# Third attention layer: a software-pipelined loop is made two steps deeper, with the head norms one step later and all that follows them two steps later

## The chip, the core and the metric

The kernel runs on one core of a Trainium2 chip, in one launch. Its time is the device time of that launch in microseconds (us). The core has five instruction streams that run side by side and meet only at semaphores: TensorE (PE in the profile; its weight loads stand apart as PEld), VectorE (DVE), ScalarE (ACT), GpSimd (POOL) and SyncE (SP). Each stream executes in the order in which it is written, so an instruction that waits holds up all that stands behind it on its engine.

## The reference, cut to what matters

The model has four layers of attention and feed-forward network (FFN) over x of 8 x 128 tokens x 256 features. The change is in the attention of the third layer (`_L2_xattn_ref`), which is:

```python
ln_out = _ln(hidden_states, ln_w, ln_b)
q  = _ln(fp8_linear(ln_out, wq), qln_w, qln_b)      # 16 heads of 128
k  = _ln(fp8_linear(ln_out, wk), kln_w, kln_b)      # 8 groups of 128
v  = fp8_linear(ln_out, wv)
core = gqa(q, k, v)                                 # softmax(q k / sqrt(128)) v
qx = _ln(fp8_linear(ln_out, wqx), qxln_w, qxln_b)
kx, vx = split(cond @ w_kv_x.T); kx = _ln(kx, kxln_w, kxln_b)
xout = gqa(qx, kx, vx)
cat = concatenate([core, xout])
return (div_clamp_fp8(cat, proj_smooth) @ wproj.T) * (proj_in_scale * proj_w_scale)
```

Each head of q, k, qx and kx is layer-normalised on its own (the head norms).

## The kernel before, in words

`attention_l2` quantises the layer's input first and then runs one long loop, in which all engines work on several **items** at once. An item is a pair (b, side): batch element b of 8, side 0 the self attention (q, k, v) and side 1 the attention over the context (qx, kx, vx). There are 16 items, in the order (0,0), (0,1), (1,0) and so on. Each item has 8 **steps** t = 0 to 7, and every engine's program goes through the same steps in the same order; `phases` (line 1345) calls each engine's `fn` with the item that enters (`pi`), the one before it (`ai`) and the one before that (`zi`), with two empty items at either end. What stands at a step is laid out by hand with a lag in steps, counted from t = 0 of `pi`:

- PE projects one block of 512 columns at each t into PSUM tile `l2x_pr` (line 1420 in bf16, six matmuls; line 1425 in f32, four matmuls, at t = 0, 1, 6, 7 of side 1).
- ACT copies it out (line 1488), to `l2x_raw` for t = 0 to 5 (two blocks of keys, four of queries) and to `v`, shown as x_normT, for t = 6, 7.
- DVE takes the moments of block t (`bn_stats`, line 1540). POOL combines them for two blocks at a time, at t = 1, 3, 5, with nine small operations and a power (lines 1389 to 1399; x^-0.5).
- `norm_due` with lag 3: DVE normalises block u at step u + 3 (line 1550, four instructions, one a head). With lag 4: PE transposes the block (line 1440) into the one tile `l2x_tr`, and ACT copies it out with the affine of the norm (line 1502) to `kT` or `qT`.
- `due` places the work of a quarter a = 0 to 3 of an item (4 heads), every second step, counted from t = 0 of `ai`: scores on PE (lag 0, line 1433), their maximum on DVE (lag 0, line 1545), exp on ACT (lag 1, line 1493), the reciprocal of the sum on DVE (lag 2, line 1556), the product with it on POOL (lag 2, line 1403), transposes of the probabilities on PE and their copy on ACT (lag 4, lines 1447 and 1507), values on PE and their copy on ACT (lag 5, lines 1454 and 1514), rounding to fp8 on DVE (lag 6, lines 1564 and 1216 to 1218) and POOL (lag 7, line 1380), and the output projection into `l2x_y` on PE (lag 9, line 1465).
- At the end of side 1 DVE adds the output to x (line 1571), behind its step 7 of `zi`.

Where several things fall on one step, each engine has a fixed order. DVE: moments, maximum, normalise, reciprocal, rounding. PE: projection, scores, transposes of the norm, transposes of the probabilities, values, output. ACT: copy of the projection, exp, affine, copy of the probabilities, copy of the values. The dual tiles (`pr`, `s`, `p`, `pT`, `of`, `step`, `wide`) are used in turns; credits (line 42) fill the semaphores beforehand.

```python
if job := norm_due(t, 4, pi, ai):
    _, u, l = job
    pe.wait_ge(s["normed"], l + 1)
    pe.wait_ge(s["affined"], l + 1)
```

Of the kernel before, what the change touches and what calls it, by code (L numbers as in the profile page):

```python
# [12 lines left out]
ALU = mybir.AluOpType  # L13
# [4 lines left out]
D = 256  # L18
KD = D // P
B = 8  # L20
# [1205 lines left out]
def attention_l2(pg, pre):  # L1226


    nc, G, DH = pg.nc, 8, 128
# [5 lines left out]
    with outer:  # L1235
# [71 lines left out]
        s = {m: pg.sem(f"l2x_{m}") for m in names}  # L1307
        with ExitStack() as st:
# [36 lines left out]
            def phases(fn):  # L1345
                items = [None, None] + [(b, side) for b in range(B) for side in range(2)] + [None, None]
                for i in range(2, len(items)):
                    fn(items[i], items[i - 1], items[i - 2])
# [8 lines left out]
            def due(t, lag, ai, zi):  # L1357

                for it, at in ((ai, t), (zi, t + 8)):
                    a, odd = divmod(at - lag, 2)  # L1360
                    if it is not None and not odd and 0 <= a < 4:
                        return it, a, item(it) * 4 + a
                return None
# [5 lines left out]
            def _(pool):  # L1369
# [5 lines left out]
                def fn(pi, ai, zi):  # L1375
                    for t in range(8):
                        if job := due(t, 7, ai, zi):
                            _, a, m = job
                            pool.wait_ge(s["widened"], m + 3)
                            nc.gpsimd.tensor_tensor(cq[:, a], wide[:, a % 2], step[:, a % 2], ALU.subtract).then_inc(s["quanted"], 1)  # L1380
# [19 lines left out]
                        if job := due(t, 2, ai, zi):  # L1400
                            _, a, m = job
                            pool.wait_ge(s["recip"], m + 1)
                            nc.gpsimd.tensor_tensor(p[:, a % 2], p[:, a % 2], rsm[:, a % 2].unsqueeze(2).to_broadcast([P, U, P]),  # L1403
                                                    ALU.mult).then_inc(s["p_normed"], 1)
# [3 lines left out]
            def _(pe):  # L1408
                def fn(pi, ai, zi):
                    for t in range(8):  # L1410
# [17 lines left out]
                        if job := due(t, 0, ai, zi):  # L1428
                            it, a, m = job
                            pe.wait_ge(s["affined"], item(it) * 6 + a + 4)  # L1430
                            pe.wait_ge(s["exped"], m + 1)
                            for j in range(U):
                                last = nc.tensor.matmul(s_ps[a % 2][:, j, :], qT[:, it[1], a, j, :], kT[:, it[1], 2 * a + j // 2, :], start=True, stop=True)
                            last.then_inc(s["scores"], 1)
                        if job := norm_due(t, 4, pi, ai):
                            _, u, l = job
                            pe.wait_ge(s["normed"], l + 1)
                            pe.wait_ge(s["affined"], l + 1)
                            for j in range(U):
                                last = nc.tensor.transpose(tr[:, j, :], raw[:, u, j, :], pg.ident[:])  # L1440
                            last.then_inc(s["ln_turned"], 1)
                        if job := due(t, 4, ai, zi):
                            _, a, m = job
                            pe.wait_ge(s["p_normed"], m + 1)
                            pe.wait_ge(s["p_kept"], m + 1)
                            for j in range(U):
                                last = nc.tensor.transpose(pt[:, j, :], p[:, a % 2, j, :], pg.ident[:])
                            last.then_inc(s["p_turned"], 1)
                        if job := due(t, 5, ai, zi):
# [7 lines left out]
                        if job := due(t, 9, ai, zi):  # L1457
# [13 lines left out]
            def _(act):  # L1471
# [8 lines left out]
                def fn(pi, ai, zi):  # L1480
                    for t in range(8):
# [7 lines left out]
                        if job := due(t, 1, ai, zi):  # L1489
# [6 lines left out]
                        if job := norm_due(t, 4, pi, ai):  # L1496
# [7 lines left out]
                        if job := due(t, 4, ai, zi):  # L1504
                            _, a, m = job
                            act.wait_ge(s["p_turned"], m + 1)
                            nc.scalar.activation(flat(pT[:, a % 2]), flat(pt[:]), ACT.Copy).then_inc(s["p_kept"], 1)
                        if job := due(t, 5, ai, zi):
# [10 lines left out]
            def _(dve):  # L1519
# [14 lines left out]
                def fn(pi, ai, zi):  # L1534
                    for t in range(8):
                        if pi is not None and t < 6:
# [5 lines left out]
                        if job := due(t, 0, ai, zi):  # L1542
# [3 lines left out]
                        if job := norm_due(t, 3, pi, ai):  # L1546
# [6 lines left out]
                        if job := due(t, 2, ai, zi):  # L1553
# [3 lines left out]
                        if job := due(t, 6, ai, zi):  # L1557
# [9 lines left out]
                    if zi is not None and zi[1] == 1:  # L1567
                        b = zi[0]
                        dve.wait_ge(s["y_done"], b + 1)
                        xb = pg.x[:, b, :]  # L1570
                        nc.vector.scalar_tensor_tensor(out=xb, in0=y[:, 0:D], scalar=yscale[:], in1=xb, op0=ALU.mult, op1=ALU.add).then_inc(s["y_added"], 1)
# [796 lines left out]
```

## Time and profile before

| | |
|---|---|
| median of 3 runs | 1958.79 us (1957.7 to 1960.71) |
| the profiled execution | 1962.16 us, of which its span 1960.4 us |
| mean granted clock of PE | 0.854 of full speed |
| the loop that is changed | from 969 to 1420 us of the span |
| one item in the middle of the loop | 26.86 us (322.3 us for 12 items) |

The span is what lies between the first and the last recorded instruction. Lines named Lnnn are lines of the kernel. "Busy" of an engine leaves its waits out; a duration in which an instruction is held up after its start is counted as busy. Other stages stand before and after the loop: the FFN of the second layer before it, a layer norm and the FFN of the third layer behind it.

### The profile page before, as it was taken

The page shows a single profiled execution, that of the slowest core. Times are in us where ns is not written, and L with a number is a line of the kernel's source. Part 1 is how long each engine was busy: PE and PEld are TensorE (multiplying, and loading weights), DVE is VectorE, ACT ScalarE, POOL GpSimd, SP SyncE. Part 2 cuts the span into 40 slices and gives each one's busy share as a digit, 9 for nine tenths or more (in the row PEclk, how much of TensorE's full clock was granted, in tenths as well). Part 3 has the DMA queues.
Part 4 walks back from the last instruction along what each step waited for, and adds up shares of the span by engine and source line. Part 5 has one row for each costly group of instructions (what it writes and reads, how often), then busy time and mean ns, then how long its engine had stood idle before and what let it go on. Part 6 is the DMA issues. An engine that isn't in the chain of part 4 may idle for free. (4 is left out here: it accounts for less than half of the span.)

```text
span 1960.4 us, 25164 instructions
## 1 busy us (share of the span) xinstructions
PE 1622.0 (83%) x8434; PEld 1001.9 (51%) x8472; DVE 1139.4 (58%) x2581; ACT 820.9 (42%) x1887; POOL 772.1 (39%) x1036
## 2 busy tenths in 40 slices
PE   6688878999686799997189999999799989837772
PEld 5323335556453455555056666666555565535551
DVE  5788872222644732424779999999832245562335
ACT  2888873110322211112477777787631111412221
POOL 0266651000200187910466777777610000016672
PEclk9755557999688799998599999999989987957896
DMA  2198871110500313110200000000011110056656
GB/s 73 44 170 164 161 152 63 41 32 25 172 1 12 146 59 127 51 62 2 85 1 2 1 2 1 2 1 1 1 59 33 41 32 1 4 209 213 212 167 236
DMA packets 174224, 140.12 MB, mean 71 GB/s; under 512 B 141793, under 2 KB 154721, under 8 KB 170386
## 3 DMA queue, kind: packets, MB, share of 16 engines
q1 hardware_dynamic: 165314, 114.89, 20.7%
q0 software_dynamic: 6416, 22.03, 3.4%
q10 hardware_dynamic: 2368, 1.61, 0.3%
q8 instruction: 69, 1.13, 0.3%
q14 instruction: 57, 0.47, 0.1%
HBM read 85.43 MB, written 19.50 MB: 54 GB/s over the span
## 5 line engine op out<-in xcount | busy, mean ns | idle before, releaser
L1811 POOL CAST l0m_pi<-l0m_pf 128x1024 bf16<-128x1024 int16 x128 | 133.2, 1040 | 136.3 <-ACT l0m_pf L1878 135.4
L350 PE MATMUL l1e_gu<-x_normT,l1e_w 128*128 128x512 f32 x384 | 170.8, 599 | 0.0
L1905 DVE TENSOR_REDUCE l0m_mx<-l0m_s 128x1 f32<-128x1024 f32 x128 | 155.8, 1217 | 25.0 <-PE l0m_s L1820 24.0
L1420 PE MATMUL l2x_pr<-l_w,l2x_xq 128*128 128x512 bf16 x538 | 134.4, 386 | 42.9 <-ACT credits L42 40.5
L1878 ACT ACTIVATE l0m_pf<-l0m_s,l0m_bias,l0x_sq 128x1024 int16<-128x1024 f32 x128 | 154.0, 1204 | 33.0 <-DVE l0m_bias L1909 26.9
L1820 PE MATMUL l0m_s<-l0x_kT,l0x_qT 48*128 48x512 bf16 x256 | 124.0, 622 | 31.9 <-ACT l0m_pf L1878 26.5
L1550 DVE TENSOR_SCALAR l2x_raw<-l2x_raw,l2x_mv,l2x_rs 128x128 f32<-128x128 f32 x384 | 147.9, 446 | 3.3 <-POOL l2x_rs L1399 3.3
L350 PE MATMUL l0e_gu<-x_normT,l0e_w 128*128 128x512 f32 x272 | 121.6, 602 | 0.0
L350 PEld LDWEIGHTS l1e_gu<-x_normT,l1e_w 128*128 128x128 f32 x384 | 73.8, 193 | 83.8 <-issue 82.8
L350 PE MATMUL l2e_gu<-x_normT,l2e_w 128*128 128x512 f32 x256 | 114.2, 601 | 0.0
L426 DVE TENSOR_TENSOR l1e_h<-l1e_sil,l1e_gu 128x512 f32<-128x512 f32 x40 | 27.5, 687 | 132.9 <-ACT l1e_sil L402 132.9
L1540 DVE BATCH_NORM_STATS2 l2x_bn<-l2x_raw 128x6 f32<-128x128 f32 x384 | 83.1, 278 | 36.2 <-ACT l2x_raw L1488 36.1
L1420 PEld LDWEIGHTS l2x_pr<-l_w,l2x_xq 128*128 128x128 bf16 x576 | 57.1, 99 | 91.6 <-ACT credits L42 40.5
L402 ACT ACTIVATE l1e_sil<-l1e_gu 128x512 f32<-128x512 f32 x48 | 28.6, 596 | 178.6 <-PE l1e_gu L350 178.6
L1403 POOL TENSOR_TENSOR x_norm<-x_norm,l2x_rsm 128x512 f32<-128x512 f32 x64 | 76.5, 1195 | 63.9 <-DVE l2x_rsm L1556 63.8
L1493 ACT ACTIVATE x_norm<-l2x_s,l2x_mx 128x128 f32<-128x128 f32 x256 | 90.0, 370 | 1.0 <-DVE l2x_mx L1545 0.9
L1380 POOL TENSOR_TENSOR l2x_cq<-ctx_tok,l2x_step 128x512 bf16<-128x512 f32 x64 | 74.2, 1159 | 38.6 <-DVE ctx_tok L1218 38.6
L1440 PE MATMUL l2x_tr<-ident,l2x_raw 128*128 128x128 f32 x384 | 61.9, 284 | 30.7 <-DVE l2x_raw L1550 30.3
L357 PE MATMUL l1e_y<-l1e_w,l1e_h 128*128 128x256 f32 x384 | 86.1, 379 | 0.0
L426 DVE TENSOR_TENSOR l0e_h<-l0e_sil,l0e_gu 128x512 f32<-128x512 f32 x28 | 19.2, 688 | 110.7 <-ACT l0e_sil L402 110.7
L350 PEld LDWEIGHTS l0e_gu<-x_normT,l0e_w 128*128 128x128 f32 x272 | 52.5, 194 | 60.0 <-issue 59.3
L357 PEld LDWEIGHTS l1e_y<-l1e_w,l1e_h 128*128 128x128 f32 x384 | 73.0, 190 | 18.5 <-issue 9.6
(515 smaller groups left out, 3635.3 us busy)
## 6 DMA issues: line engine op xcount, KB each, us to landing
l3m_w<-in_l_moe SPq DMA_DIRECT2D x16, 1280.0 KB, 6.7
l1e_w<-in_l_ffn SPq DMA_DIRECT2D x24, 384.0 KB, 3.2
l_rows<-zero_row SPq DMA_DIRECT2D x8, 1024.0 KB, 11.1
l_w<-l_rows SPq DMA_DIRECT2D x8, 1024.0 KB, 11.9
l0e_w<-in_l_ffn SPq DMA_DIRECT2D x17, 384.0 KB, 3.1
l2e_w<-in_l_ffn SPq DMA_DIRECT2D x16, 384.0 KB, 3.1
ctx_tok<-l_route SPq DMA_DIRECT2D x8, 512.0 KB
l2q_wps<-in_l_wp SPq DMA_DIRECT2D x16, 256.0 KB, 2.8
```

Source lines behind the costliest of these rows:

```text
L350: last = nc.tensor.matmul(gu[half][:, m, :], w[:, c % SW, (2 * k + m) * P:(2 * k + m + 1) * P], pg.xnT[:, k, cols(n)], start=(k == 0), sto ...
L357: last = nc.tensor.matmul(y[:, t, :], h[:, c % SH, t * P:(t + 1) * P], w[:, c % SW, WG:CHUNK], start=(c == 0 and t % 2 == 0), stop=False, ...
L1380: nc.gpsimd.tensor_tensor(cq[:, a], wide[:, a % 2], step[:, a % 2], ALU.subtract).then_inc(s["quanted"], 1)
L1403: nc.gpsimd.tensor_tensor(p[:, a % 2], p[:, a % 2], rsm[:, a % 2].unsqueeze(2).to_broadcast([P, U, P]), ALU.mult).then_inc(s["p_normed"], 1)
L1420: last = nc.tensor.matmul(flat(pr[t % 2][:]), src[:, k, tokens], pg.l2_w3[:, part, k, at:at + W], start=(k == 0 and part == 0), stop=(k == ...
L1493: last = nc.scalar.activation(p[:, a % 2, j, :], s_ps[a % 2][:, j, :], ACT.Exp, bias=mx[:, a % 2, j:j + 1], accum_out=sm[:, a % 2, j:j + 1])
L1540: last = nc.vector.bn_stats(bn[:, t, j, :], raw[:, t, j, :])
L1550: last = nc.vector.tensor_scalar(raw[:, u, j, :], raw[:, u, j, :], mv[:, u, j, 0:1], rs[:, 1, u, j:j + 1], ALU.subtract, ALU.mult)
L1811: nc.gpsimd.tensor_copy(pi[:, n % 8, :], pf[:, n % 4, :]).then_inc(s["rounded"], 1)
L1820: last = nc.tensor.matmul(s_ps[n % 3][:, g * HALF:(g + 1) * HALF], qT[:, h, b * P:(b + 1) * P], kT[:, h, g * HALF:(g + 1) * HALF], start=T ...
L1878: nc.scalar.activation(pf[:, n % 4, :], s_ps[n % 3][:], ACT.Exp, scale=sq[:, b, h:h + 1], bias=bias[:, n % 4:n % 4 + 1], accum_out=sm[:, b ...
L1905: nc.vector.tensor_reduce(mx[:, n % 4:n % 4 + 1], s_ps[n % 3][:], AX, ALU.max).then_inc(s["maxed"], 1)
```

## The change

Every lag of `due` on every engine is raised by 2, so that scores, softmax, values, rounding and output of an item come two steps later against its projections. Of the head norms, DVE's normalise goes from lag 3 to lag 4, and PE's transposes and ACT's affine from lag 4 to lag 6. The last lag is then 11 and its last quarter falls at step 17 of `ai`, so a fourth item `wi` is handed through, and there are three empty items at either end. DVE's addition to x moves from behind step 7 of `zi` to the start of step 2 of `wi`. No instruction, tile or buffer is added or taken away. The head of every `fn` gets the fourth argument.

```diff
             def phases(fn):
-                items = [None, None] + [(b, side) for b in range(B) for side in range(2)] + [None, None]
-                for i in range(2, len(items)):
-                    fn(items[i], items[i - 1], items[i - 2])
+                items = [None] * 3 + [(b, side) for b in range(B) for side in range(2)] + [None] * 3
+                for i in range(3, len(items)):
+                    fn(items[i], items[i - 1], items[i - 2], items[i - 3])
...
-            def due(t, lag, ai, zi):
+            def due(t, lag, ai, zi, wi):
...
-                for it, at in ((ai, t), (zi, t + 8)):
+                for it, at in ((ai, t), (zi, t + 8), (wi, t + 16)):
...
             def _(pool):
...
-                        if job := due(t, 7, ai, zi):
+                        if job := due(t, 9, ai, zi, wi):
...
-                        if job := due(t, 2, ai, zi):
+                        if job := due(t, 4, ai, zi, wi):
...
             def _(pe):
...
-                        if job := due(t, 0, ai, zi):
+                        if job := due(t, 2, ai, zi, wi):
...
-                        if job := norm_due(t, 4, pi, ai):
+                        if job := norm_due(t, 6, pi, ai):
...
-                        if job := due(t, 4, ai, zi):
+                        if job := due(t, 6, ai, zi, wi):
...
-                        if job := due(t, 5, ai, zi):
+                        if job := due(t, 7, ai, zi, wi):
...
-                        if job := due(t, 9, ai, zi):
+                        if job := due(t, 11, ai, zi, wi):
...
             def _(act):
...
-                        if job := due(t, 1, ai, zi):
+                        if job := due(t, 3, ai, zi, wi):
...
-                        if job := norm_due(t, 4, pi, ai):
+                        if job := norm_due(t, 6, pi, ai):
...
-                        if job := due(t, 4, ai, zi):
+                        if job := due(t, 6, ai, zi, wi):
...
-                        if job := due(t, 5, ai, zi):
+                        if job := due(t, 7, ai, zi, wi):
...
             def _(dve):
...
                     for t in range(8):
+                        if wi is not None and wi[1] == 1 and t == 2:
+                            b = wi[0]
+                            dve.wait_ge(s["y_done"], b + 1)
+                            xb = pg.x[:, b, :]
+                            nc.vector.scalar_tensor_tensor(out=xb, in0=y[:, 0:D], scalar=yscale[:], in1=xb, op0=ALU.mult, op1=ALU.add).then_inc(s["y_added"], 1)
...
-                        if job := due(t, 0, ai, zi):
+                        if job := due(t, 2, ai, zi, wi):
...
-                        if job := norm_due(t, 3, pi, ai):
+                        if job := norm_due(t, 4, pi, ai):
...
-                        if job := due(t, 2, ai, zi):
+                        if job := due(t, 4, ai, zi, wi):
...
-                        if job := due(t, 6, ai, zi):
+                        if job := due(t, 8, ai, zi, wi):
...
-                    if zi is not None and zi[1] == 1:
-                        b = zi[0]
-                        dve.wait_ge(s["y_done"], b + 1)
-                        xb = pg.x[:, b, :]
-                        nc.vector.scalar_tensor_tensor(out=xb, in0=y[:, 0:D], scalar=yscale[:], in1=xb, op0=ALU.mult, op1=ALU.add).then_inc(s["y_added"], 1)
```

## Rows read from the trace of the kernel before

**Rows 1.** Windows: busy time of each engine in 12 items of the loop

```profile
core 0: us, PE busy (x) PEld busy (x) DVE busy (x) ACT busy (x) POOL busy (x), PEclk, DMA share, GB/s
1069.00:1391.30 322.30, 300.02 (x1746) 209.68 (x1773) 296.98 (x872) 252.40 (x794) 235.61 (x456) 1.00 0.00 1
```

**Rows 2.** Who waited for whom, 1069 to 1391.3 us: total, times, longest

```profile
PEld l2x_tr L1440 <- DVE l2x_raw L1550: 38.1, 48, 1.3
...
DVE l2x_bn L1540 <- ACT l2x_raw L1488: 20.0, 24, 1.2
PE l2x_tr L1440 <- DVE l2x_raw L1550: 19.8, 24, 1.1
```

**Rows 3.** The same for steps 0+1, 2+3, 4+5, 6+7 of one side-1 item

```profile
1149.66:1156.51 6.85, 6.80 (x41) 4.75 (x41) 5.67 (x18) 5.44 (x19) 2.22 (x2) 1.00 0.00 0
1156.51:1161.76 5.25, 5.25 (x34) 3.77 (x34) 4.37 (x16) 4.30 (x16) 4.86 (x13) 1.00 0.01 2
1161.76:1169.34 7.58, 6.55 (x36) 4.25 (x36) 7.48 (x23) 5.69 (x19) 6.56 (x14) 1.00 0.01 2
1169.34:1176.59 7.25, 7.17 (x44) 5.18 (x44) 7.08 (x19) 5.38 (x19) 6.01 (x12) 1.00 0.00 0
```

**Rows 4.** The same for the whole side-0 item behind it

```profile
1176.59:1203.39 26.80, 24.36 (x148) 17.08 (x149) 24.89 (x73) 21.26 (x67) 19.62 (x38) 1.00 0.00 1
```

**Rows 5.** Timeline of PE around that item's step 4, and at a step 0

```profile
1163.23 0.66 PE L1440 MATMUL l2x_tr<-ident,l2x_raw 128*128 128x128 f32 x4 [0.97 <-DVE l2x_raw L1550]
1163.72 0.60 PE L1447 MATMUL l2x_pt<-ident,x_norm 128*128 128x128 f32 x4
...
1203.93 0.60 PE L1440 MATMUL l2x_tr<-ident,l2x_raw 128*128 128x128 f32 x4
1204.37 0.60 PE L1447 MATMUL l2x_pt<-ident,x_norm 128*128 128x128 f32 x4
```

**Rows 6.** DVE alone, between the maxima of steps 0, 2, 4, 6, 0

```profile
1151.14:1158.08 6.94, 5.66 (x19) 1.00 0.00 0
1158.08:1163.88 5.80, 5.70 (x20) 1.00 0.01 1
1163.88:1170.23 6.35, 6.18 (x19) 1.00 0.01 3
1170.23:1178.15 7.92, 7.18 (x19) 1.00 0.00 0
```

**Rows 7.** Timeline: DVE's normalise and POOL's wide operations in the same stretches

```profile
1160.19 1.24 POOL L1403 TENSOR_TENSOR x_norm<-x_norm,l2x_rsm 128x512 f32<-128x512 f32 x1
1161.23 1.94 DVE L1550 TENSOR_SCALAR l2x_raw<-l2x_raw,l2x_mv,l2x_rs 128x128 f32<-128x128 f32 x4
1161.39 1.19 POOL L1380 TENSOR_TENSOR l2x_cq<-ctx_tok,l2x_step 128x512 bf16<-128x512 f32 x1
...
1168.78 1.39 DVE L1550 TENSOR_SCALAR l2x_raw<-l2x_raw,l2x_mv,l2x_rs 128x128 f32<-128x128 f32 x4
...
1170.84 1.11 DVE L1550 TENSOR_SCALAR l2x_raw<-l2x_raw,l2x_mv,l2x_rs 128x128 f32<-128x128 f32 x4
```

**Rows 8.** Timeline from the exp of one step 1 to the next exp, ACT and DVE

```profile
1207.21 0.36 ACT L1493 ACTIVATE x_norm<-l2x_s,l2x_mx 128x128 f32<-128x128 f32 x1
...
1210.24 0.75 ACT L1488 ACTIVATE l2x_raw<-l2x_pr,l2c_scales 128x512 f32<-128x512 f32 x1
1211.03 0.87 DVE L1540 BATCH_NORM_STATS2 l2x_bn<-l2x_raw 128x6 f32<-128x128 f32 x4 [1.17 <-ACT l2x_raw L1488]
1211.82 0.67 DVE L1545 TENSOR_REDUCE l2x_mx<-l2x_s 128x4 f32<-128x512 f32 x1
```

**Rows 9.** Timeline: the addition to x on DVE

```profile
1176.26 0.47 DVE L1571 SCALAR_TENSOR_TENSOR x_res<-l2x_y,l2x_yscale,x_res 128x256 f32<-128x256 f32 x1
```

**Rows 10.** A pair of steps while the loop fills, and two pairs while it drains

```profile
991.22:998.22 7.00, 6.78 (x39) 4.23 (x38) 3.36 (x13) 5.30 (x14) 1.99 (x10) 1.00 0.00 0
1397.91:1405.08 7.17, 5.80 (x42) 4.86 (x41) 6.21 (x13) 6.04 (x26) 3.73 (x4) 1.00 0.00 1
```

More of the change, by code:

```diff
@@ L1373, in _, with fn @@
                 AGGR = 9
-                def fn(pi, ai, zi):
+                def fn(pi, ai, zi, wi):
                     for t in range(8):
-                        if job := due(t, 7, ai, zi):
+                        if job := due(t, 9, ai, zi, wi):
                             _, a, m = job
@@ L1408, in _, with fn @@
             def _(pe):
-                def fn(pi, ai, zi):
+                def fn(pi, ai, zi, wi):
                     for t in range(8):
@@ L1478, in _, with fn @@
                 act.wait_ge(s["smooth"], 1)
-                def fn(pi, ai, zi):
+                def fn(pi, ai, zi, wi):
                     for t in range(8):
@@ L1532, in _, with fn @@
                 QSTEPS = 3
-                def fn(pi, ai, zi):
+                def fn(pi, ai, zi, wi):
                     for t in range(8):
+                        if wi is not None and wi[1] == 1 and t == 2:
[3 more added lines that the diff above has]
+                            nc.vector.scalar_tensor_tensor(out=xb, in0=y[:, 0:D], scalar=yscale[:], in1=xb, op0=ALU.mult, op1=ALU.add).then_inc(s["y_added"], 1)
                         if pi is not None and t < 6:
```

## The prediction

> **What bounds the kernel now.** I read the page's tenths first, to find where this loop lies, and then three views of it: busy time by windows, the waits, and the timeline. In the middle of the loop 12 items take 322.3 us, 26.86 us each, with PE busy for 300.02 us (25.0 an item) and DVE for 296.98 us (24.75), while ACT and POOL have more room, and the granted clock is 1.00 [rows 1]. So no engine is full, but two are within 8% of it: what is lost is 1.86 us an item on PE and 2.1 us on DVE. The waits say how. PE waits 24 times, 19.8 us in all (1.65 us an item), to transpose a block that DVE has not yet normalised; its weight loads wait 38.1 us for the same. DVE waits 24 times, 20.0 us, for ACT's copy of a projection, and that copy comes from PE [rows 2]. The two hold each other up.
>
> The place shows by pairs of steps. Steps 2 and 3 carry no transposes of a norm and take 5.25 us, with PE busy all the time. Steps 4 and 5 take 7.58 us, of which PE works 6.55 [rows 3]. The missing 0.97 us is the wait of the first transpose, at 1163.23 us [rows 5]. It stands for the normalise that began at 1161.23 and took 1.94 us [rows 7]. PE wants the block one step after DVE may begin it, and DVE reaches each step some 2 us after PE.
>
> **The change, part by part.** All work keeps its amount; only its distance in steps changes.
>
> *Transposes 2 steps behind the normalise instead of 1.* This adds a step, some 3.2 us (26.86 / 8 is 3.36), to a distance that lacks 0.97 us now, so 2.2 us are left over and PE's 1.65 us an item go. What is late next: the transposes of the probabilities wait for POOL's product. In the same pair of steps the product ends at 1160.19 + 1.24 = 1161.43 us [rows 7] and PE takes it at 1163.72 [rows 5], after its own 0.97 us of waiting. Without that wait 1.3 us of slack is left. This is enough for the mean, not for every disturbance.
>
> *Normalise one step later.* The steps of DVE that carry one change from 0, 3, 4, 5, 6, 7 to 0, 1, 4, 5, 6, 7. Counted from maximum to maximum DVE is busy 5.66, 5.70, 6.18 and 7.18 us [rows 6]. The four instructions of a normalise take 1.11 us undisturbed, 1.03 in a row with others (0.08 overlaps), and 0.28 more where they meet the end of a POOL operation (1.39) [rows 7]. The first stretch becomes 5.66 + 1.03 + 0.28 = 6.97 us. The second loses the disturbed one of 1.94 us: 3.76 us. So the load becomes less even: 6.97, 3.76, 6.18, 7.18.
>
> *What keeps DVE from using the light stretch.* Exp needs the maximum, and on ACT the exp, the affine and the copy of the values stand ahead of the next projection's copy, which DVE's moments and next maximum need. From the exp at 1207.21 us it goes to the copy at 1210.24, the moments at 1211.03, the maximum at 1211.82 plus 0.67 [rows 8]: 5.28 us, with 0.1 us for the handover 5.4 us. No stretch can be shorter. DVE's round is then 6.97 + 5.4 + 6.18 + 7.18 = 25.73 us in an item with the addition to x, and 0.4 less in one without (it takes 0.47 us [rows 9], less the overlap).
>
> *PE's round.* Its transposes move from steps 0, 1, 4 to 7 to steps 0 to 3, 6, 7; the amount stays. They cost 0.44 us a block (1203.93 to 1204.37 us) [rows 5]. PE is busy 6.80 + 5.25 + 6.55 + 7.17 = 25.77 us in a side-1 item [rows 3] and 24.36 us in a side-0 item [rows 4].
>
> *The sum an item.* Side 1: the larger is PE's 25.77. Side 0, into which the addition to x now falls (step 2 of `wi`): DVE's 25.73. The mean is 25.75. To it I add 0.2 us, what PE waits today for other causes (1.86 - 1.65). That gives **25.95 us an item** against 26.86: 0.91 us less, and over the 15 items that enter with scores running 13.7 us less.
>
> *The addition to x, moved.* It waits for PE's last output matmul. Before, PE issues that in step 7 and DVE adds behind its own step 7. Now they are step 1 and the head of step 2, and PE's next use of the tile is at step 3 where it was step 1: the same distances. It costs nothing, since DVE runs behind PE: the present one starts with no wait [rows 9]. If DVE caught up with PE it would wait at most for that group of matmuls, under 1 us every second item, with the moments, the maximum and all of DVE's step 2 behind it.
>
> *Depth.* The loop has two steps more. One pair of the fill stays without scores. Such a pair was 7.00 us when the first scores fell into it, PE busy 6.78 [rows 10]; without its scores and the load of exp's table I take 4.6 (bounds 4.0 and 7.0). One full pair of 26.86 / 4 = 6.7 us goes, and the drain gains a pair: two of them take 7.17 us [rows 10], 3.6 each. That is 4.6 - 6.7 + 3.6 = +1.5 us. Norms and transposes that now reach further into the drain add about 1 us (one normalise of 1.03 us exposed; bounds 0 and 2). Together +2.5 us, between +0.4 and +6.
>
> **Sum:** -13.7 + 2.5 = -11.2 us. Against the profiled execution of 1962.2 us (span 1960.4 and 1.8 around it) this gives 1951.0. That execution lies 3.4 us over the median of the runs, 1958.8, so for a median I predict **1947.6 us**.
>
> **A rule to set beside the rows.** The normalise of four instructions takes 1.11 us undisturbed and 1.94 us while POOL's product (1160.19 to 1161.43 us) and rounding (from 1161.39) run [rows 7]; DVE stands still meanwhile, and its busy time holds that. The Trainium skill (SBUF — State Buffer, section "SBUF: two separate sides") says that DVE and GpSimd share a port pair which one of them holds for a whole instruction while the other is blocked. By that rule a DVE without gaps meets more of POOL's operations. The trace agrees with the block itself (1.94 against 1.11 us).
>
> **The rivals.**
>
> *A. The wait simply goes.* PE's 1.65 us an item vanish and DVE keeps up: 25.2 us an item. 15 x 1.65 = 24.8 us less, 2.5 more: 1936.5 us. For it: PE's other waits are small [rows 1, 2]. Against it: DVE's 24.75 us busy would have to fit almost without a gap. Chance 0.17.
>
> *B. POOL in DVE's way.* DVE's gaps (20.0 us in 12 items [rows 2]) now let POOL's rounding pass. If they go, the normalises of steps 1 and 5 are held for 0.83 us each (1.94 - 1.11) instead of 0.28: 1.1 us an item more on DVE. With PE partly above it in side 1, some 0.65 of it reaches the item: 26.6 us, 15 x 0.26 = 3.9 less, 2.5 more: 1957.4 us, no change that can be told. The rule above would work this way. Against it: at step 1 today DVE has a gap of 1.17 us [rows 8] that POOL may use, and part of it stays, as the light stretch is bound by ACT. Chance 0.18.
>
> *C. Slower: the uneven rounds don't even out.* PE and DVE may stay tied pair by pair, now by POOL's product (1.3 us slack). Then each pair costs the larger of the two. PE's side-1 pairs become 6.80, 6.11, 5.69, 7.17 (two transposes of 0.43 moved from the third to the second), and DVE's are 6.97, 5.4, 6.18, 7.18: the maxima sum to 26.44. The same sum for today is 6.80 + 5.70 + 6.55 + 7.18 = 26.23, and the item really takes 26.93 [rows 3], 0.7 more. If those 0.7 remain, the item takes 27.14 us: 0.28 more, x 15 = 4.2, and 2.5 for depth: 1965.5 us. It decides from the point where DVE cannot be 2 us behind PE after steps 4 to 1 without PE waiting. For it: DVE's heavy stretches now follow each other (6.18, 7.18, 6.97), 20.3 us in which PE needs 19.7. Against it: 1.3 us of slack covers that difference of 0.6. Chance 0.15.
>
> **How the numbers follow.** My forecast has 0.50, with a range of its own from 1942 to 1954: the depth's bounds give -2 and +3.5, and 0.2 us more or less an item 3 each way. About 0.2% (4 us) is what a measurement of this kernel can tell from no change: the border of faster is 1954.9, of slower 1962.7. Faster: the forecast, A, and 0.04 of B's spread, less 0.01 of the forecast's own tail, 0.70. Slower: C, 0.15. The same: the rest, 0.15. The range from 1936 to 1961 takes in A's centre, the forecast and B, and leaves out C (0.15) and what lies below A's centre (some 0.05).
>
> **What would show it.** Right: in the waits, "PE l2x_tr for DVE l2x_raw L1550" falls from 24 in 12 items to a handful. Steps 4 and 5 come down from 7.6 us to about 6, while steps 2 and 3 rise from 5.25 us to about 6. DVE's stretch from step 2 to 4 is the one with an idle time (about 1.6 us), waiting for ACT; an item takes about 26 us. The last maximum to the end of the loop is unchanged, the drain one pair longer. B would show as more than 1.39 us for the normalises of steps 1 and 5, with DVE busy over 25.5 us an item; C as PE waiting for POOL L1403 at its transposes of the probabilities. I am wrong if an item stays near 26.9 us, or if the waits for the normalise remain.

## The result: 1927.8 us, 31 us faster

| | before | after |
|---|---|---|
| median | 1959.22 us (1957.70 to 1960.71, 4 runs) | 1927.78 us (1926.58 to 1929.21, 4 runs) |
| ratio | | 0.9837 (95% interval 0.9822 to 0.9851) |
| profiled execution | 1962.16 us, span 1960.4 | 1926.58 us, span 1924.8 |
| the loop, first projection to last addition | 451.5 us | 427.3 us |
| 12 items in its middle | 322.4 us | 305.7 us |
| its first three items | 73.1 us | 60.9 us |
| its last item and the drain | 56.0 us | 60.6 us |
| the rest of the span | 1508.9 us | 1497.5 us |

The direction was forecast, the size was not: I gave 1947.6 us, from 1936 to 1961. The loop alone gave 24.2 us where 11.2 were forecast, and the profiled executions differ by a further 11.4 us in stages that the change doesn't touch. An item is counted from the start of ACT's first copy (line 1488) of it to that of the next, except that the first one begins with the loop.

The middle of the loop after the change, busy time by engine (the columns of [rows 1]), and its waits:

```profile
1025.60:1331.30 305.70, 296.58 (x1747) 209.86 (x1777) 285.35 (x870) 253.12 (x794) 236.37 (x457) 1.00 0.00 1
```

```profile
DVE l2x_bn L1545 <- ACT l2x_raw L1488: 15.4, 12, 1.3
PEld l2x_tr L1440 <- DVE l2x_raw L1555: 14.1, 24, 1.2
ACT x_norm L1493 <- DVE l2x_mx L1550: 12.7, 18, 1.2
...
PE l2x_tr L1440 <- DVE l2x_raw L1555: 5.3, 12, 0.7
...
PE l2x_pt L1447 <- POOL x_norm L1403: 1.8, 6, 0.3
```

PE is busy 97% of the time, against 93% in [rows 1]. Its wait for the normalise (now line 1555; the moments are line 1545 and the maximum line 1550) fell from 19.8 us to 5.3 us. DVE is busy 11.6 us less for nearly the same instructions, mainly because they are held up for less time after their start: the normalises take 5.9 us less (below) and the last step of the rounding (line 1218) 3.5 us less.

DVE alone between the maxima of the steps that were 0, 2, 4, 6 and 0 in [rows 6] (now 2, 4, 6, 0 and 2), over two items:

```profile
1130.33:1137.31 6.98, 6.88 (x24) 1.00 0.01 2
1137.31:1142.61 5.30, 3.91 (x16) 1.00 0.00 2
1142.61:1148.66 6.05, 5.95 (x20) 1.00 0.00 0
1148.66:1155.46 6.80, 6.70 (x20) 1.00 0.01 2
1155.46:1162.84 7.38, 7.28 (x25) 1.00 0.00 1
1162.84:1168.14 5.30, 3.91 (x15) 1.00 0.01 3
1168.14:1174.50 6.36, 6.26 (x19) 1.00 0.00 0
1174.50:1181.31 6.81, 6.71 (x20) 1.00 0.00 0
```

The second stretch is the light one: 3.91 us of work in 5.30 us, each time. All others are full. So DVE sets the pace, except in that stretch, where its next moments wait for ACT.

### The profile page after: what moved, and what is told of

It is laid out like the page before. It is cut to its first block and busy times, and to the rows that moved or that the text cites. A ratio compares the mean times of both kernels' runs of the same rounds, so it can differ in the third digit from the quotient of the medians.

```text
span 1924.8 us, 25164 instructions
## 1 busy us (share of the span) xinstructions
PE 1602.1 (83%) x8434; PEld 993.4 (52%) x8472; DVE 1120.4 (58%) x2581; ACT 821.3 (43%) x1887; POOL 773.6 (40%) x1036
## 5 line engine op out<-in xcount | busy, mean ns | idle before, releaser
L1555 DVE TENSOR_SCALAR l2x_raw<-l2x_raw,l2x_mv,l2x_rs 128x128 f32<-128x128 f32 x384 | 141.7, 429 | 1.6 <-POOL l2x_rs L1399 1.5
L350 PE MATMUL l0e_gu<-x_normT,l0e_w 128*128 128x512 f32 x272 | 121.7, 602 | 0.0
L1399 POOL TENSOR_TENSOR l2x_rs<-l2x_rs,l2x_half 128x8 f32<-128x8 f32 x48 | 83.4, 1737 | 3.8
```

What stands on the lines that cost most here:

```text
L350: last = nc.tensor.matmul(gu[half][:, m, :], w[:, c % SW, (2 * k + m) * P:(2 * k + m + 1) * P], pg.xnT[:, k, cols(n)], start=(k == 0), sto ...
L1399: g.tensor_tensor(rs[:, 1, two, :], var, half[:, 0], ALU.pow).then_inc(s["rstd"], 1)
L1555: last = nc.vector.tensor_scalar(raw[:, u, j, :], raw[:, u, j, :], mv[:, u, j, 0:1], rs[:, 1, u, j:j + 1], ALU.subtract, ALU.mult)
```

## The experiments

The ratios are to the kernel before, run in the same group. The groups of runs differ: the kernel before took 1957.5, 1977.3, 1957.9 and 1979.9 us (medians) in the four of them. In r_before 18 us of this lie behind the first matmul of the fourth layer's expert stage (264.1 us to the end, against 246.1 us in the first profile); the cause is open. So kernels of different groups are compared by ratio, and by the time of their loop.

| run | ratio, 95% interval | loop | first 3 items | 12 items | rest |
|---|---|---|---|---|---|
| kernel before | 1 | 451.5 | 73.1 | 322.4 | 56.0 |
| changed kernel | 0.9837 [0.9822, 0.9851] | 427.3 | 60.9 | 305.7 | 60.6 |
| e1 depth only | 1.0004 [0.9989, 1.0019] | 451.8 | 71.6 | 322.4 | 57.7 |
| e2 transposes at lag 5, no depth | 0.9939 [0.9923, 0.9956] | 440.0 | 65.6 | 318.1 | 56.2 |
| e3 normalise 3, transposes 6 | 0.9900 [0.9884, 0.9917] | 433.1 | 61.6 | 312.0 | 59.5 |
| e4 normalise 4, transposes 5 | 1.0009 [1.0000, 1.0019] | 461.1 | 70.3 | 328.6 | 62.1 |
| r_before | 0.9998 [0.9988, 1.0009] | 450.1 | 73.1 | 322.5 | 54.5 |
| r_after | 0.9829 [0.9811, 0.9847] | 427.3 | 60.9 | 305.7 | 60.7 |
| e5 normalise 4, transposes 7 | 0.9886 [0.9866, 0.9906] | 426.1 | 60.0 | 305.6 | 60.5 |
| e6 normalise 5, transposes 7 | 0.9891 [0.9874, 0.9907] | 429.3 | 61.5 | 307.6 | 60.2 |
| e7 one short memset more | 0.9889 [0.9872, 0.9907] | 427.5 | 60.9 | 305.9 | 60.7 |
| e8 six memsets more | 0.9854 [0.9836, 0.9873] | 427.4 | 60.9 | 305.8 | 60.7 |
| e9 normalise 3, moments first | 1.0105 [1.0087, 1.0123] | 474.5 | 66.6 | 348.5 | 59.4 |
| e10 one step of depth | 0.9935 [0.9902, 0.9967] | 438.2 | 67.4 | 313.0 | 57.8 |
| e11 normalise 3, no power | 0.9820 [0.9793, 0.9846] | 417.7 | 59.6 | 300.1 | 58.0 |
| e12 changed kernel, no power | 0.9852 [0.9832, 0.9872] | 427.3 | 60.8 | 305.7 | 60.8 |

### Which of the three moves makes the gain

**Depth alone (e1).** The lags of `due` as in the change, the head norms as before:

```diff
-                        if job := norm_due(t, 4, pi, ai):   # DVE
+                        if job := norm_due(t, 3, pi, ai):
-                        if job := norm_due(t, 6, pi, ai):   # PE, ACT
+                        if job := norm_due(t, 4, pi, ai):
```

> Only the lags of scores to output are raised by 2 and the fourth item is in flight; normalise stays at lag 3, transposes and affine at lag 4. Theory (the distance between normalise and transposes makes the gain): PE still waits for DVE's normalise some 1.6 us an item, an item stays at 26.7 to 27.0 us, and the kernel takes about 1958 to 1962 us. Rival (the depth itself, more distance between projections and scores, makes the gain): an item falls to 25.5 us and the time to about 1930 us.

The 12 items take 322.4 us, the same as before to 0.1 us, with the same waits:

```profile
PEld l2x_tr L1440 <- DVE l2x_raw L1555: 38.1, 48, 1.3
...
PE l2x_tr L1440 <- DVE l2x_raw L1555: 19.9, 24, 1.1
DVE l2x_bn L1545 <- ACT l2x_raw L1488: 19.1, 24, 1.2
```

So depth gives nothing by itself, and costs little: the loop is 0.3 us longer (1.5 less in the fill, 1.7 more at the end), or 1.7 us against the loop of r_before, which had a faster end (54.5 us).

**Depth and the later normalise, but the old distance of one step (e4).** `norm_due(t, 5, ...)` on PE and ACT in the changed kernel.

> The changed kernel with transposes and affine at lag 5, one step behind the normalise as before the change. Theory (distance): PE's waits for the normalise come back (15 us or more in 12 items), an item takes 26.5 to 27.2 us, the time 1948 to 1962 us. Rival (depth or the new place of the normalise makes the gain): an item stays near 25.5 us, the time near 1930 us.

The waits are back, worse than before the change, and 12 items take 328.6 us. The upper end that I gave, 27.2 us an item, was still too low (27.4):

```profile
PEld l2x_tr L1440 <- DVE l2x_raw L1555: 44.4, 48, 1.6
DVE l2x_bn L1545 <- ACT l2x_raw L1488: 35.3, 24, 2.1
...
PE l2x_tr L1440 <- DVE l2x_raw L1555: 25.8, 36, 1.1
```

e1 and e4 together show that the gain stands or falls with the second step between normalise and transposes. Depth is its room: at transposes of lag 6 block 2 is turned at step 0 of `ai`, and PE's scores of the first quarter, which need it, would stand ahead of it at the old lag 0.

**The distance alone, without depth (e2).** The kernel before with one edit, on PE and ACT:

```diff
-                        if job := norm_due(t, 4, pi, ai):
+                        if job := norm_due(t, 5, pi, ai):
```

> The kernel before with one edit: transposes and affine at lag 5 instead of 4, that is two steps behind the normalise, no extra depth; the affine of a quarter's last block is then one step ahead of its scores instead of two. Theory (distance makes the gain): an item falls to 25.2 to 25.7 us, and the time to 1926 to 1940 us. Rival (the distance from the affine to the scores is needed as well): PE waits for ACT's copy l2x_qT at its scores (L1433), an item stays above 26.3 us, the time above 1948 us.

The kernel gains 0.6%, where the change gains 1.6%, and neither account holds: the time is 1945.77 us and an item takes 26.5 us, but not for the reason that the rival gave. The waits in its middle 12 items name another engine:

```profile
PE l2x_pt L1447 <- POOL x_norm L1403: 14.2, 12, 1.5
...
DVE l2x_raw L1550 <- POOL l2x_rs L1399: 12.3, 12, 1.0
```

PE now waits for POOL's product, and DVE's normalise waits for POOL's power. Neither wait stands in the middle of the loop in the kernel before.

### Why the normalise has to be later too

**Normalise back at lag 3 (e3),** the rest as in the change:

```diff
-                        if job := norm_due(t, 4, pi, ai):   # DVE
+                        if job := norm_due(t, 3, pi, ai):
```

> The changed kernel with DVE's normalise back at lag 3, transposes at lag 6 (three steps apart). Theory of the prediction (moving the normalise makes DVE's load uneven, and the light stretch from the maximum of step 2 to that of step 4 idles 1.3 us): the idle time in that stretch goes, an item falls from 25.5 to about 25.1 us, the time by some 5 us to 1922. Rival (the disturbances by POOL grow where the normalise then falls, at step 3): an item stays at 25.5 us or above and the time at 1928 us or above.

The first account, the prediction's, fell: 12 items take 312.0 us, 6.3 more than with lag 4. The rival's range came (26.0 us an item, 1937.88 us), but its reason, POOL's disturbances, is only a part. The timeline of POOL, DVE and PE in steps 2 to 4 of a side-1 item shows why:

```profile
1088.91 0.21 POOL L1389 TENSOR_TENSOR l2x_rs<-l2x_bn 128x8 f32<-128x8 f32 x1
...
1091.78 1.64 POOL L1399 TENSOR_TENSOR l2x_rs<-l2x_rs,l2x_half 128x8 f32<-128x8 f32 x1
...
1093.38 1.04 POOL L1403 TENSOR_TENSOR x_norm<-x_norm,l2x_rsm 128x512 f32<-128x512 f32 x1
1093.45 2.68 DVE L1555 TENSOR_SCALAR l2x_raw<-l2x_raw,l2x_mv,l2x_rs 128x128 f32<-128x128 f32 x4 [1.03 <-POOL l2x_rs L1399]
1094.38 1.16 POOL L1380 TENSOR_TENSOR l2x_cq<-ctx_tok,l2x_step 128x512 bf16<-128x512 f32 x1
1094.47 0.66 PE L1447 MATMUL l2x_pt<-ident,x_norm 128*128 128x128 f32 x4 [0.92 <-POOL x_norm L1403]
```

POOL combines the moments of steps 0 and 1 from 1088.91 us on, and its power ends at 1093.42. DVE has reached step 3 by then and has waited 1.03 us. POOL's product, whose reciprocal was ready at 1089.9 us, stood behind the power too, and PE waits 0.92 us for it. Then DVE's four instructions meet the product and the rounding and take 2.68 us instead of 1.11.

**Is it POOL's power, or DVE's collisions?** In e9 I put POOL's combination of the moments ahead of its rounding at the same step.

> The run with normalise at lag 3 and transposes at lag 6 (312.0 us for 12 items, PE waiting 13.3 us for POOL's product) with one edit more: POOL combines the moments ahead of its rounding at the same step, instead of behind it. Theory (with normalise at lag 3 the faster loop is held by POOL's combination of moments, which ends in its power and stands before both DVE's normalise at step 3 and POOL's own product): that chain starts some 0.4 us sooner (the moments were ready at 1088.4 us and POOL began at 1088.9), and 12 items take 2 to 6 us less than 312.0. Rival (the cost of lag 3 is DVE's uneven load and its collisions): 12 items stay at 312 us or grow, since the rounding comes later to PE.

The first fell: 348.5 us for 12 items. The rival's range came, but by its side remark: the rounding now stands behind the power, and PE waits for it at the output projection, 30.9 us in some 250 us of the loop (its clock also fell to half four times for 3.4 us in these items). An edit that hands the delay to another consumer doesn't tell the two causes apart. So the power's time itself was taken away, at lag 3 (e11) and at lag 4 (e12). These kernels leave out the reciprocal of the standard deviation; all else stays:

```diff
-                            g.tensor_tensor(rs[:, 1, two, :], var, half[:, 0], ALU.pow).then_inc(s["rstd"], 1)
+                            g.tensor_tensor(rs[:, 1, two, :], var, half[:, 0], ALU.mult).then_inc(s["rstd"], 1)
```

> Normalise at lag 3, transposes at lag 6, and POOL's power (x^-0.5, 1.64 us, 3 an item) replaced by a product of the same tiles (about 0.2 us), so that the standard deviations are not computed and the time alone is read. Theory (POOL's combination of moments holds DVE's normalise at step 3 and its own product behind it): the waits for l2x_rs and for POOL's product go, and 12 items take 303 to 307 us instead of 312.0. Rival (DVE's collisions and uneven load cost at lag 3): 12 items stay at 310 us or more.

> The changed kernel with the power replaced in the same way. Theory (at lag 4 POOL's combination is hidden already): 12 items take 303 to 306 us instead of 305.7, so at most half of what the same edit gives at lag 3. Rival (POOL holds the loop at lag 4 as well): 12 items take under 302 us.

At lag 3 it gives 11.9 us in 12 items (312.0 to 300.1, below the 303 that I gave as the lower end), at lag 4 nothing (305.7 both). Without the power, at lag 3 and at lag 4:

```profile
1029.30:1329.30 300.00, 297.82 (x1755) 211.44 (x1784) 295.07 (x871) 251.75 (x793) 183.94 (x456) 1.00 0.00 1
```

```profile
1030.00:1335.70 305.70, 295.36 (x1748) 208.66 (x1778) 294.93 (x871) 253.39 (x793) 181.32 (x456) 1.00 0.00 1
```

```profile
DVE l2x_bn L1545 <- ACT l2x_raw L1488: 5.8, 12, 0.6
```

So POOL's power is what lag 3 costs once PE no longer waits elsewhere. That lag 4 hides it is seen best in the waits: DVE waits 6 times, 6.2 us, for `l2x_rs` in e3 and never in the 12 items of the changed kernel. The 305.7 us of e12 are a net value, for the edit also moves POOL's product onto DVE's line 1216, which takes 49.5 us there against 22.8, and DVE is busy 9.6 us more in all. And the prediction's own argument is in e11 and e12: DVE is busy alike (295.07 and 294.93 us), but at lag 4 it waits 5.8 us for ACT's copy and at lag 3 not at all, which is about the 5.6 us between them. It is the smaller of two effects.

**More distance (e5, e6).** Transposes at lag 7; in e6 the normalise at lag 5 as well.

> The changed kernel with transposes and affine at lag 7, three steps behind the normalise. Theory (two steps are enough, since DVE and ACT set the pace): PE's last waits for the normalise (5.3 us in 12 items) go, but an item stays at 25.3 to 25.5 us, the time within 3 us of the changed kernel. Rival (the remaining waits still cost): an item falls to 25.0 us, the time by 5 us or more.

> The changed kernel with both moved one step further: normalise at lag 5, transposes and affine at lag 7. The distance of two steps stays, and the distance of the normalise to POOL's power grows. DVE's steps with a normalise are then 0 to 2 and 5 to 7. Theory (lag 4 already hides POOL's power, and what counts beyond that is where the normalise falls against the other work of DVE): no wait for POOL's l2x_rs here either, the light stretch moves from step 2 to 4 to the stretch from 2 to 6, an item takes 25.3 to 26 us, no gain. Rival (more distance from POOL still pays): an item falls below 25.2 us.

e5: 305.6 us in 12 items, as with lag 6. PE's waits for the normalise are gone, and it gives nothing, since DVE and ACT set the pace. Its median missed what I gave: 1954.50 us is 8.9 more than r_after's in the same group, though the loop is 1.2 us shorter; most of it is in the clock, told below. e6: 307.6 us, no gain either.

**Half the depth (e10).** All lags of `due` one lower than in the change.

> The changed kernel with scores and all that follows one step sooner (lags 1, 3, 5, ... 10: one step deeper than before the change, not two), normalise at lag 4 and transposes at lag 6 as in the change; the addition to x one step sooner. Theory (the distance between normalise and transposes makes the gain, depth is only the room for it, and the affine one step ahead of its scores is enough): an item takes 25.3 to 25.8 us, fill and drain half a pair less, and the loop is within 3 us of the 427.3 us of the changed kernel. Rival (the place of the scores against the other work counts: scores, maximum, reciprocal and rounding now fall on the odd steps on which POOL also combines the moments): an item takes over 26 us.

The theory fell: 12 items take 313.0 us, the loop 438.2. Its waits in the middle:

```profile
DVE l2x_bn L1545 <- ACT l2x_raw L1488: 22.0, 24, 1.6
PEld l2x_pt L1447 <- POOL x_norm L1403: 20.3, 24, 1.4
DVE l2x_mx L1550 <- PE l2x_s L1433: 18.9, 12, 2.0
```

The scores and what follows them now share their steps with other neighbours. DVE collides much less (busy 266.5 us in 12 items, 18.9 less than in the changed kernel), and waits more. The range that the rival gave (over 26 us an item) is what came. Which of the shifted neighbours does it was not taken apart.

### The part of the gain outside the loop

The kernel before and the changed one, unchanged, once more in another group of runs:

> The kernel before, unchanged, once more. In the first profiles the changed kernel is 35.6 us shorter, of which the loop gives 24.2 us, and 11.4 us lie in stages that the change doesn't touch (4.5 before the loop, 6.7 in the fourth layer's attention, whose first 20.5 us ran at half of PE's clock in the kernel before and only 6.8 us in the changed one). Theory (the outside part varies from one execution to the next, as the clock does): the outside part of this execution, 1508.9 us then, comes out several us different, and the loop takes 451.5 us again within 0.5. Rival (it belongs to the kernel): 1508 to 1510 us outside, and again some 20 us at half clock.

> The changed kernel, unchanged, once more, on the same chip as the kernel before. Theory (outside varies): the loop takes 427.3 us within 0.5, the outside part, 1497.5 us in the first profile, differs by several us, and the two kernels' medians differ by 24 to 30 us. Rival (it belongs to the kernel): 1496 to 1499 us outside and medians 31 us or more apart.

The changed loop repeats (427.3 us). That of the kernel before takes 450.1 us, 1.4 less than before and outside the 0.5 that I allowed; the difference is in its end, where PE's clock stood at half for 3.4 us in the first profile and not in this one. The medians are again 30.5 us apart (1976.10 and 1945.62; 31.7 by all runs of the kernel before in the group, 1977.33), so 6 to 9 us beyond the loop's 23 to 24 come back in the medians. The two profiled executions are only 23.9 us apart: outside the loop they take 1520.4 and 1519.3 us, since this time the changed kernel entered its loop 4.7 us later. So neither account came whole.

What returns in both pairs lies where the clock does. I count from the last matmul of line 350, the gate and up projection of the third layer's FFN; 13.8 us of matmuls of line 357 follow it (the expectation of e7 calls it the FFN's last matmul, which it isn't), and then PE is idle for 6.7 us, in which the clock falls. These are the windows that begin 17 us behind that matmul (PEclk stands third from the end), of the kernel before:

```profile
1605.30:1612.30 7.00, 3.42 (x14) 2.76 (x15) 6.15 (x28) 4.69 (x10) 0.00 (x0) 0.50 0.42 140
1612.30:1626.30 14.00, 13.22 (x44) 9.61 (x43) 9.76 (x17) 2.26 (x3) 2.86 (x19) 0.52 0.04 11
```

and of the changed one:

```profile
1576.80:1583.80 7.00, 3.42 (x14) 2.77 (x15) 6.16 (x28) 4.69 (x10) 0.00 (x0) 0.51 0.42 140
1583.80:1597.80 14.00, 13.22 (x58) 7.99 (x57) 11.95 (x22) 2.26 (x3) 2.86 (x19) 1.00 0.04 11
```

Both run the same instructions after the same idle stretch. Before, PE stays at 1.2 GHz (0.5) for 20.5 us; after, it is back at 2.4 GHz after 6.8 us. From that matmul to the first of the fourth layer's expert stage it is 126.0 us before (123.6 in r_before) and 118.9 us after, in both of its profiles. All 16 profiles sort by the moment at which the clock fell behind that matmul: at 16.5 to 16.9 us the stretch takes 125.8 to 126.0 us (the kernel before, e5, e6), at 17.0 to 17.2 us 118.9 to 119.9 us (the changed kernel twice, e4, e8, e12), at 17.3 to 17.8 us 123.3 to 123.6 us (r_before, e1, e2, e3, e7, e9, e10, e11).

Is the 118.9 the changed kernel's own, or a moment that it happens to hit? e7 and e8 add memsets on DVE behind the loop:

```diff
                 phases(fn)
+                nc.vector.memset(z[:], 0.0)          # e7; e8: raw[:, u] for u in range(6)
```

> The changed kernel with one short extra DVE instruction behind the loop (a memset of the dead tile z, 512 bf16 columns, some 0.1 to 0.3 us). Between the end of the third layer's FFN and the fourth layer's expert stage the profiles so far show 118.9 us where the granted clock fell 17.0 us after the FFN's last matmul (both profiles of the changed kernel), 125.7 to 126.0 us where it fell at 16.5 to 16.9 us, and 123.3 to 123.5 us at 17.3 to 17.8 us. Theory (what the change gains outside the loop is the clock's step, hit or missed by where the loop ends): the clock now falls 0.1 to 0.5 us sooner against the stage, the stretch takes 126 us, and the kernel is 5 to 7 us slower than the changed one, for an instruction of 0.3 us or less. Rival (the changed kernel has these 7 us for itself): 118.9 us again, the time 0.3 us more.

> The changed kernel with six extra DVE memsets of 512 f32 columns behind the loop (some 1.5 to 3.5 us). Theory (the clock's step): the time grows by those us plus or minus up to 7 us, according to the moment at which the clock falls; the stretch behind the FFN takes one of the values seen, 118.9, 123.5 or 126 us, and it follows that moment as in the other profiles. Rival: the stretch keeps 118.9 us whatever that moment is, and the time grows by the length of the memsets alone.

The one memset takes 0.27 us. The stretch is at 123.3 us again, 4.4 us longer, and from the loop's end to the FFN's last matmul of line 350 it is 2.9 us more (170.8 against 167.9 us), of which 0.27 are the memset: 7.3 us for an instruction of 0.27. In that first part too the clock differs: behind the loop it stood at half for 23.9 us on end, and in the changed kernel for 10.3 and 6.8 us with 3.4 us at full between. The median is 1936.68 us against 1927.78. The six memsets take 2.9 us and cost less than the one: the median is 1931.16 us, with the stretch back at 118.9 us. The window of 14 us that shows it, of e7 and of e8:

```profile
1587.70:1601.70 14.00, 13.22 (x50) 8.51 (x49) 10.78 (x19) 2.26 (x3) 2.86 (x19) 0.75 0.04 11
```

```profile
1590.10:1604.10 14.00, 13.22 (x58) 7.97 (x57) 11.95 (x22) 2.26 (x3) 2.86 (x19) 1.00 0.06 11
```

E8's six memsets move the stages by another amount, and the clock fell 17.0 us behind that matmul, as in the changed kernel; in e7 it fell at 17.4. The expected 126 us for e7 was wrong in its value (the clock fell later, not sooner), but the claim held for this stretch: what the change gains there is a moment hit, and one instruction of 0.27 us takes it away. Only one execution of each run was profiled, so for the 6 to 9 us in the medians the clock is the likely cause, not one that was followed in every execution.

## Why the prediction was wrong, step by step

**What bounds the kernel: right.** PE's wait for the normalise was the cause. It fell from 19.8 to 5.3 us in 12 items, and only the runs with two or more steps between normalise and transposes gained anything. Two signs came as given: steps 4 and 5 of a side-1 item came down from 7.58 to 5.52 us, and steps 2 and 3 rose from 5.25 to 6.09. The waits fell to 12, not to a handful.

**The stretches of DVE: right to 0.4 us.** Forecast 6.97, 5.4, 6.18, 7.18. Measured 6.98, 5.30, 6.05 and 6.80, and in the item behind 7.38, 5.30, 6.36, 6.81. The light stretch bound by ACT came as worked out, with its idle time of 1.4 us. The 7.18 us still held the addition to x, which now runs at 1161.66 us, in the 7.38 us: it moved from one stretch to another and changes no sum.

**The sum an item: 25.95 forecast, 25.48 measured.** Two terms were too large. The first is "the larger of the two engines, item by item": PE's 25.77 us of a side-1 item, read while PE still waited, are no bound. In the changed kernel PE is busy 25.35 us in such an item (1125.35 to 1150.89 us) and 24.11 in the one behind it, 24.7 in the mean (296.58 / 12). DVE's round for both, 25.73 and 0.4 less, gives 25.53, near what came. Why PE's side-1 work reads 0.4 us less was not taken apart. The second is the 0.2 us for PE's other waits: e5 took PE's waits for the normalise away as well and gained nothing. Over 15 items the two and the rest are 7 us.

**Depth: +2.5 us forecast, +0.3 or +1.7 measured (e1).** Of the 2.5, 1 us was for the norms, which e1 leaves in place. Of the other 1.5, the fill gave back 1.5 us where I had 2.1 (4.6 - 6.7), and the end cost 1.7 us against the first profile of the kernel before and 3.2 against r_before, where I had 3.6. The first profile lost time at its end that the other two didn't:

```profile
1393.60:1397.00 3.40, 3.40 (x14) 2.67 (x13) 2.09 (x4) 2.73 (x12) 2.12 (x2) 0.50 0.00 0
```

So this term was near.

**What failed: the fill.** I gave the first three items the gain of the steady loop, 0.91 us each from the second on, and 2.1 us for the pair without scores, 3.9 us in all. They gave 12.2 us, and the end lost 4.6 where I had 3.7. This is the larger part of the miss: 8.3 us, against 5.8 in the 12 middle items (16.7 us where I had 10.9). Depth alone gives 1.5 of the 12.2 (e1), the distance of the transposes most of the others: 61.6 us in e3 against 71.6 in e1. While the loop fills (966 to 1042.2 us of the kernel before), PE waits for the normalise 7.9 us in 8 waits, the first of them 2.9 us, against at most 1.1 in the middle; in the fill of the changed kernel 0.5 us are left:

```profile
PEld l2x_tr L1440 <- DVE l2x_raw L1550: 12.3, 11, 3.4
...
PE l2x_tr L1440 <- DVE l2x_raw L1550: 7.9, 8, 2.9
```

```profile
PE l2x_tr L1440 <- DVE l2x_raw L1555: 0.5, 2, 0.3
```

At the end of the first of the 8 waits PE's clock fell for 3.4 us, which the changed one didn't see. The windows are of the kernel before and of the changed one, whose clock is 1.00 from there to the end of the fill:

```profile
980.60:984.00 3.40, 3.06 (x10) 1.62 (x11) 2.09 (x10) 0.78 (x1) 2.59 (x6) 0.50 0.00 0
```

```profile
976.00:980.70 4.70, 4.33 (x20) 2.40 (x21) 3.84 (x17) 2.83 (x5) 4.15 (x15) 1.00 0.00 0
```

My waits had been read from 1069 us on, and the fill's were never priced. What the clock's fall has of the 12.2 us was not measured apart; r_before and e1 saw it in their fills too (73.1 and 71.6 us), e3 did not.

**Moving the normalise: the sign was wrong.** I priced it as a loss through uneven load. At the same distance or more, lag 3 is 6.3 us slower in 12 items than lag 4 (e3), because it exposes POOL's power. I had named POOL as the next wait, and its slack as 1.3 us, but only for the product, and never asked when the power is ready for DVE's normalise, because [rows 2] shows no such wait. It showed none since DVE came late to step 3 in the kernel before: the power ended at 1160.23 us, and the normalise began at 1161.23 [rows 7].

**The rivals.** A (the wait simply goes) came nearest with 1936.5 us, and its reason is half right: 25.2 us an item were forecast, 25.48 came, and it left out the fill too. B (POOL in DVE's way) fell: DVE is busy 23.8 us an item, not over 25.5. The normalises took 115.4 us before and 109.5 after, since the one that collided at step 3 (2.45 and 1.94 us) now runs at step 4, undisturbed:

```profile
L1550 DVE TENSOR_SCALAR l2x_raw<-l2x_raw,l2x_mv,l2x_rs 128x128 f32<-128x128 f32 x289 | 115.4, 459 | 0.0
```

```profile
L1555 DVE TENSOR_SCALAR l2x_raw<-l2x_raw,l2x_mv,l2x_rs 128x128 f32<-128x128 f32 x288 | 109.5, 439 | 0.0
```

Of the sign that I gave for B, one in four came: the normalise of step 5 of a side-1 item takes 1.94 us, the other three of steps 1 and 5 take 1.38 to 1.39. At lag 3 they all take 121.7 us in the same number of items. The rule of the Trainium skill on the shared port (SBUF — State Buffer, "SBUF: two separate sides") agrees with the single collisions here (2.68 us for four instructions in e3). It holds for some of DVE's operations only, and the moments were not held up (0.86 us at 1160.45 us, below). That a DVE without gaps meets more of POOL's operations, as I took from it, didn't come here: in a pair of items 6 of 12 normalises are held up before and after, 1.1 us less in all. C (pairs stay tied) is refuted in the changed kernel, where PE waits 1.8 us for POOL's product in 12 items, but its mechanism shows in e2 (14.2 us) and e3 (13.3 us).

**Outside the loop:** nothing forecast, 7 us in the medians and 11.4 us between the two profiles. These 7 us are luck, and not what the miss rests on: with the loop's gain alone the median would be 1935.0 us (1936.4 by the loop of r_before), at the edge of my range, and that gain is twice the 11.2 us forecast. The 4.5 us of these before the loop are variation between executions (the loop began at 969.1 us in one profile of the kernel before and at 964.5 in the other).

## What to carry to other kernels

When a wait between two engines is taken away, price it in the fill and drain too, where a single one can be longer (2.9 us here against 1.1), and ask of every producer on the way when its result is ready at the new pace, for a wait that the profile doesn't show may be hidden by the one that you remove. Judge a change by the time of its own stretch first: a gain of some us elsewhere can be a moment of the clock that the next edit loses.

## What the runs showed of the hardware

PE's granted clock makes the time outside a change depend on when that change ends, and not in order: 0.27 us of extra work cost 7.3 us in the two stages behind it and 8.9 us in the median, 2.9 us of extra work cost 3.2 us in the same two stages and 3.4 us in the median (e7, e8). The medians are of different groups of runs; the ratios, 0.9889 and 0.9854 against 0.9837, are in the same order. The same stretch took 118.9 to 119.9, 123.3 to 123.6 or 125.8 to 126.0 us with the same instructions, by the moment at which the clock fell in the idle time ahead of it and by how long it stayed at the lower level (6.8, twice 6.8, or 20.5 us). In the loop itself the clock stood at 1.00 in both kernels except for its first 4.6 us, 3.4 us in the fill of the kernel before, and 3.4 us in the end of each (from 1393.6 and 1365.2 us) besides the last 3 us.

An instruction of DVE can be held up after its start by one of POOL, and it depends on which. Beside POOL's product or rounding the four instructions of a normalise take up to 2.69 us instead of 1.10, and line 1216 takes 1.01 us instead of 0.29; in e12 it begins at 1149.28 us, 0.27 us behind the product. The moments at 1160.45 us in the kernel before take their usual 0.86 us beside the same product. And beside POOL's power of 1.64 us on 128x8 neither of two instructions was held up: in the kernel before the power runs from 1158.59 to 1160.23 us, and line 1216 at 1159.18 us takes its 0.29 us; in e3 a normalise at 1097.42 us takes 1.10 us, with the power from 1097.70 us on.
